# Three gate products in banks of their own, and the attention inputs' scale and bias on other engines

## The chip, the core and the metric

One core of one Trainium2 chip runs the whole program. The metric is the device time of one execution in microseconds (us), the median of three runs. All data are fp32 unless said otherwise.

## The reference, cut to what matters

The input x has 8 batches, 512 time steps and 256 features; a conditioning vector has 256 features per batch. Four layers are added to x one after the other. The first two are recurrences over the 512 steps, and they are what the change touches, with the projections that begin the third:

```
x = x + rnn(x, cond)      # h = tanh(x_t Wx + b + h Wh)
x = x + lstm(x, cond)     # a = x_t Wx + b + h Wh; i, f, o = sigmoid of three quarters, g = tanh of the last
                          # c = f * c + i * g;  h = o * tanh(c)
x = x + attention(x, cond)  # hyperbolic: layer_norm(logmap0(x)), expmap0, then q, k, v =
                            # logmap0(xm) @ w + b, heads, softmax, a feed-forward layer
x = x + experts(x, cond)  # gating over 4 experts, the best 2 of them, and a shared one
```

In the kernel logmap0(xm) @ w is written as s1 * (z @ w): the row factor s1 comes out of the norm of z, and the bias is added behind it.

## The kernel before, in words

The program has two blocks. The first holds both recurrences, with all that prepares the attention beside them; the second holds attention and experts, batch by batch, and the diff leaves it alone.

**The recurrences** (`recurrences`) run in 520 slots. Slot i does step i of the RNN and step n = i - 8 of the LSTM (`LAG` = 8). A state has 256 units for 8 batches. The products turn it round: the state is the stationary operand, 8 to 32 columns wide, and the weights stream past it in four strips of 32 array columns (`products`, tile_position (0, 32 j)), so the result lies on 128 partitions. Each slot issues for the LSTM a product for the forget and input gates into psFI (128 wide), one for the candidate into psG (64 wide), and a joint one for the output gate and the RNN into psOR. At 32 rows per group of four slots, a bank serves four steps: its stationary operand grows from 8 to 32 columns, and the four steps' bias (copied by ScalarE, `bias_of_group`, `bias_of_pair`) and input products (`inputs_of_group`, `inputs_of_pair`) are put in ahead.

VectorE transposes the results in 32x32 blocks back to units on partitions (FIT, GT, oT, RT), multiplies f * c (line 240, `gw<-sFI,cc`), makes the new cell state with one scan (line 243), and multiplies o * tanh(c) into Hs (line 250) and once more into RH (line 251).
```
dve.wait_ge(sem["w"], n + 1)      # line 241: f * c is there
dve.wait_ge(sem["tG"], n + 1)     # line 242: tanh of the candidate is there
dve.tensor_tensor_scan(...)       # line 243
```

After its LSTM and RNN work each engine does one slot's worth of side work (`inputs_made(i)`, and `Q.scalar_slot` or `Q.vector_slot` for the first batch's heads).

**The attention's inputs** (`AttentionInputs`) are that side work. A chunk is 16 steps of 8 batches, 128 rows; 32 chunks follow each other 16 slots apart. o counts a chunk's slots from 0, and two chunks overlap (o = 16 + p of one is o = p of the next). PE transposes the rows back (o = 0, 1), ScalarE copies them (o = 1), VectorE takes the moments (o = 2: bn_stats, bn_aggr) and clips (o = 5), GpSimd computes an inverse tanh with pow and a polynomial (up to line 907, signal d; after VectorE's group at o = 9, which ends with line 841, up to line 921, signal rstd), VectorE centres and scales (o = 13, 14), ScalarE sums the squares of z (o = 15, line 620), GpSimd takes the root (line 924, signal nz), VectorE makes the row factor s1 (`row_factors`, o = 20, lines 687 to 693), PE transposes z (o = 18, 19) and multiplies it with w_q, w_k, w_v (o = 20 to 31, one 128x128 product per slot, line 782). VectorE then writes each third, psB * s1 + bias, to the tile qkv (o = 23, 27, 31, line 856), and SP stores the chunk. `row_factors` in chunks after `GATHERED` = 24 has one more wait ahead of its reciprocal (line 689).

The line numbers in this document are those of the kernel before, also for instructions that the change keeps. 

Of the kernel before, what the change touches and what calls it, by code (L numbers as in the profile page):

```python
# [9 lines left out]
fp32 = mybir.dt.float32  # L10
# [7 lines left out]
P = 128  # L18
# [47 lines left out]
class Recurrence:  # L66
# [14 lines left out]
    SIGNALS = ("FI", "G", "OR", "XX", "X1", "sFI", "tG", "sO", "tR", "tC", "bFI", "bG", "bOR", "fiT", "gT", "rT", "w", "c",  # L81
# [3 lines left out]
    def __init__(self, nc, ctx, mem):  # L85
# [13 lines left out]
        self.FIT, self.GT, self.RT = sb("FIT", [P, 2 * KC, 32]), sb("GT", [P, KC, 32]), sb("RT", [P, KC, 32])  # L99
# [3 lines left out]
        self.psFI, self.psOR = ([ps(f"{n}{i}", 128) for i in range(2)] for n in ("psFI", "psOR"))  # L103
        self.psG = [ps(f"psG{i}", 64) for i in range(2)]
# [3 lines left out]
def recurrences(nc, R, F, Q, A, W):  # L108
# [5 lines left out]
    F_I, G_, O_, R_, O_R = slice(0, 128), slice(128, 192), slice(192, 256), slice(256, 320), slice(192, 320)  # L114
# [13 lines left out]
    with nc.Block() as block:  # L128

        @block.tensor  # L130
        def _(pe):
# [27 lines left out]
            def inputs_of_group(g, bank, cols, seeded, raises=None):  # L159
                q = g - FIRST  # L160
                if not 0 <= q < PIECES:
                    return
                pe.wait_ge(sem[seeded], q + 1)
# [4 lines left out]
                last = products(bank[g % 2], lambda k: x[:, k, :], 32, R.wx, cols)  # L168
                if raises:
                    last.then_inc(sem[raises], 1)  # L170
# [4 lines left out]
            for bank in R.psOR + R.psFI + R.psG:  # L175
# [6 lines left out]
            for i in range(SLOTS):  # L182
                g, s, n = i // 4, i % 4, i - LAG
                if lstm(i):
# [3 lines left out]
                    products(R.psFI[g % 2], h, width, R.wh, F_I).then_inc(sem["FI"], 1)  # L188
# [30 lines left out]
        def _(dve):  # L219
# [9 lines left out]
            for i in range(SLOTS):  # L229
                g, s, n = i // 4, i % 4, i - LAG  # L230
                at_pair = 2 * NB * (i % 2)
                if lstm(i):
                    dve.wait_ge(sem["FI"], n + 1)
                    dve.transpose(flat(R.FIT), R.psFI[g % 2]).then_inc(sem["fiT"], 1)  # L234
                    dve.wait_ge(sem["G"], n + 1)
                    dve.transpose(flat(R.GT), R.psG[g % 2]).then_inc(sem["gT"], 1)
                    dve.wait_ge(sem["sFI"], n + 1)
# [3 lines left out]
                    dve.wait_ge(sem["w"], n + 1)  # L241
                    dve.wait_ge(sem["tG"], n + 1)
# [53 lines left out]
        def _(act):  # L296
# [26 lines left out]
            for i in range(SLOTS):  # L323
# [12 lines left out]
                if rnn(i):  # L336
                    act.wait_ge(sem["rT"], i + 1)
                    act.activation(r_of(i), R.RT[:, :, at_pair:at_pair + NB], ACT.Tanh).then_inc(sem["tR"], 1)  # L338
                if s == 0:
                    bias_of_group(g + 1, R.psFI, F_I, "bFI")  # L340
# [4 lines left out]
                else:  # L345
# [3 lines left out]
                inputs_made(i)  # L349
                Q.scalar_slot(act, i)  # L350
# [95 lines left out]
class AttentionInputs:  # L446
# [14 lines left out]
    SIGNALS = {"xT": 1, "xT_out": 1, "mv": 1, "X2": 1, "n": 1, "m": 1, "d": 1, "dk": 1, "rstd": 1, "z": 1, "zz": 1, "nz": 1, "zT": 1, "zT_out": 1, "qkv": 3, "qkv_out": 3,  # L461
               "x_st": 16, "qkv_st": 16}

    def __init__(self, nc, ctx, mem, A, W, x_dram, qkv_dram, ada_dram, mod_dram, last_rows):
# [13 lines left out]
        self.psA, self.psB = (mem.enter_context(nc.psum_tensor(n, [P, 512], fp32)) for n in ("psA", "psB"))  # L478
# [88 lines left out]
    def last_bank(self, n, banks):  # L567
        return (self.psB, banks[4], banks[5])[n][:, 0:D]

    def last_rows_back(self, pe, x2, x2_made):  # L570
        c = NCH - 1
        pe.wait_ge(x2_made, 4 * (c + 1))
        pe.wait_ge(*self.at("zT_out", c - 2))
# [109 lines left out]
    def row_factors(self, dve, c):  # L683
# [10 lines left out]
        if c < NCH - 2:  # L694
            C.link(made)
# [33 lines left out]
    def tensor_engine(self, pe, x2, x2_made):  # L729
        def slot(i):  # L730
# [7 lines left out]
            if 12 <= i < 24:  # L738
# [3 lines left out]
                if (half, k) == (0, 0):  # L742
                    if j == 1:
# [1567 lines left out]
```

## Time and profile before

| | |
|---|---|
| median of 3 runs | 2344.58 us (2342.88 to 2344.84) |
| the profiled execution | 2343.05 us, its span 2341.3 us |
| mean granted TensorE clock | 0.991 |
| busy: PE, VectorE, ScalarE, GpSimd | 94%, 68%, 54%, 24% of the span |
| LSTM steps | 512 |

Engines in the rows: PE is TensorE's matrix products, DVE is VectorE, ACT is ScalarE, POOL is GpSimd; a q behind a name is the engine's queue, an instruction that keeps it waiting but does no work. A row of the timeline gives start, duration, engine, line, operation, output<-inputs and the shapes; `x16` means sixteen instructions merged, from the first start to the last end. PE products are pipelined, so a group's duration is longer than the distance to the next group's start.

### The profile page before, as it was taken

Reading aid. Unit: us, or ns where it says so; the run is one execution under the profiler, and the core shown is the slowest. Engines: PE = TensorE matmul, PEld = TensorE weight load, DVE = VectorE, ACT = ScalarE, POOL = GpSimd, SP = SyncE. Lnnn points to the kernel's source line nnn. Section 1 sums busy time; section 2 is a strip of 40 time slices with the busy share of each in tenths; the row PEclk is TensorE's granted clock in tenths of the full one; section 3 lists DMA queues with packets and bytes.
Section 4 is the critical chain, followed back from the end, with each engine's and each line's share of the span. In section 5 each row is a group of like instructions: output and inputs, shape, how many; then the busy total and the mean of one; then the engine's idle time right before and its main releaser. Section 6 shows DMA issues by size and latency. Waiting matters only on the chain. (4 is left out here: it accounts for less than half of the span.)

```text
span 2341.3 us, 94850 instructions
## 1 busy us (share of the span) xinstructions
PE 2207.2 (94%) x39004; PEld 1452.3 (62%) x39004; DVE 1581.1 (68%) x7316; ACT 1257.8 (54%) x4381; POOL 560.5 (24%) x1178
## 2 busy tenths in 40 slices
PE   8899999999999999999987699999999999999999
PEld 6677777777777777777743256464646556464666
DVE  5777777777777777777747684765747576674530
ACT  4555555555555555555565664647575564656432
POOL 0222222242221422214223031322213131221100
PEclk9999999999999999999998899999999999999999
DMA  4111111101000000000010200303030120302020
GB/s 119 36 38 31 38 40 42 37 25 32 29 31 27 22 27 29 31 27 18 23 69 1 88 35 1 131 1 131 1 131 1 38 94 1 131 1 104 0 86 9
DMA packets 51874, 102.64 MB, mean 44 GB/s; under 512 B 10468, under 2 KB 33380, under 8 KB 47348
## 3 DMA queue, kind: packets, MB, share of 16 engines
q1 hardware_dynamic: 48036, 94.06, 11.8%
q8 instruction: 309, 5.06, 0.9%
q10 hardware_dynamic: 3408, 2.52, 0.4%
q14 instruction: 121, 0.99, 0.1%
HBM read 75.53 MB, written 21.04 MB: 41 GB/s over the span
## 5 line engine op out<-in xcount | busy, mean ns | idle before, releaser
L135 PE MATMUL psFI<-wh,Hs 128*8 128x128 f32 (+3 forms) x8192 | 324.7, 276 | 61.0 <-DVE Hs L250 47.8
L135 PE MATMUL psOR<-wh,RH 128*16 128x128 f32 (+3 forms) x8320 | 321.5, 272 | 2.2 <-ACT RH L338 2.0
L135 PEld LDWEIGHTS psFI<-wh,Hs 128*8 128x8 f32 (+3 forms) x8192 | 182.2, 99 | 179.3 <-DVE Hs L250 179.3
L2054 ACT ACTIVATE pexp<-bank 128x1024 f32<-128x1024 f32 x256 | 244.3, 1023 | 36.1 <-PE bank L1384 35.9
L338 ACT ACTIVATE RH<-RT 128x16 f32<-128x16 f32 x512 | 110.9, 217 | 261.5 <-DVE RT L254 261.5
L1262 PE MATMUL bank<-x3T,ew 128*128 128x512 f32 x512 | 238.7, 593 | 0.0
L234 DVE STREAM_TRANSPOSE FIT<-psFI 128x128 f32<-128x128 f32 x512 | 162.0, 316 | 101.0 <-PE psFI L135 98.4
L329 ACT ACTIVATE sFI<-FIT 128x32 f32<-128x32 f32 x512 | 118.6, 232 | 200.4 <-DVE FIT L234 195.5
L135 PE MATMUL psG<-wh,Hs 128*8 128x64 f32 (+3 forms) x8192 | 208.6, 219 | 0.4 <-issue 0.4
L135 PEld LDWEIGHTS psOR<-wh,RH 128*16 128x16 f32 (+1 forms) x8320 | 205.7, 104 | 4.8 <-ACT RH L338 3.7
L1276 PE MATMUL bank<-ew,hidden 128*128 128x256 f32 x864 | 201.0, 379 | 0.0
L1276 PEld LDWEIGHTS bank<-ew,hidden 128*128 128x128 f32 x864 | 163.5, 190 | 56.5 <-issue 38.7
L1962 ACT ACTIVATE hidden<-bank,eb1s 128x512 f32<-128x512 f32 x128 | 87.8, 686 | 198.1 <-PE bank L1262 195.8
L2126 POOL TENSOR_TENSOR hs<-hs,half 128x16 f32<-128x16 f32 x32 | 92.8, 2901 | 378.0 <-DVE hs L1801 378.0
L782 PE MATMUL psB<-wqkv,zrT 128*128 128x128 f32 x720 | 175.8, 326 | 0.0
L135 PEld LDWEIGHTS psG<-wh,Hs 128*8 128x8 f32 (+3 forms) x8192 | 174.8, 100 | 0.6 <-issue 0.6
L135 PE MATMUL psOR<-wx,XX 128*32 128x128 f32 (+1 forms) x4160 | 168.9, 278 | 2.6 <-DMA XX<-in_xT 2.6
L335 ACT ACTIVATE tC<-cc 128x16 f32<-128x16 f32 x512 | 111.3, 217 | 105.6 <-DVE cc L243 104.8
L782 PEld LDWEIGHTS psB<-wqkv,zrT 128*128 128x128 f32 x720 | 107.1, 188 | 72.9 <-issue 70.4
L1262 PEld LDWEIGHTS bank<-x3T,ew 128*128 128x128 f32 x512 | 96.3, 190 | 77.0 <-issue 72.2
L250 DVE TENSOR_TENSOR Hs<-oT,tC 128x16 f32<-128x16 f32 x512 | 90.2, 176 | 75.8 <-ACT tC L335 1.4
L240 DVE TENSOR_TENSOR gw<-sFI,cc 128x16 f32<-128x16 f32 x512 | 90.4, 176 | 72.4 <-ACT sFI L329 3.0
(366 smaller groups left out, 4227.9 us busy)
## 6 DMA issues: line engine op xcount, KB each, us to landing
ew<-in_ew SPq DMA_DIRECT2D x32, 1024.0 KB, 9.1
qkv_scratch<-qkvr SPq DMA_DIRECT2D x31, 384.0 KB, 2.8
big<-qkv_scratch SPq DMA_DIRECT2D x7, 1536.0 KB, 7.8
XX<-in_xT SPq DMA_DIRECT2D x31, 256.0 KB, 2.7
x_scratch<-xr SPq DMA_DIRECT2D x32, 128.5 KB, 2.4
x<-x_scratch SPq DMA_DIRECT2D x8, 514.0 KB, 9.7
ada<-ada_scratch SPq DMA_DIRECT2D x8, 512.0 KB, 8.5
out_x<-x SPq DMA_DIRECT2D x7, 512.0 KB, 3.3
```

The source lines that it names most:

```text
L135: last = pe.matmul(bank[32 * j:32 * j + width, :], state(k), weights[:, k, j, cols], start=False, stop=k == KC - 1, tile_position=(0, 32 * ...
L234: dve.transpose(flat(R.FIT), R.psFI[g % 2]).then_inc(sem["fiT"], 1)
L240: dve.tensor_tensor(second_scan(R.gw), second_scan(R.sFI[:, 0]), second_scan(R.cc), ALU.mult).then_inc(sem["w"], 1)
L250: dve.tensor_tensor(h_alone(i), o, R.tC[:, :, :], ALU.mult).then_inc(sem["hL"], 1)
L329: act.activation(R.sFI[:, :, :, 1].rearrange("p g (k b) -> p (g k) b", k=KC), R.FIT[:, :, at_four:at_four + NB], ACT.Sigmoid).then_inc(sem ...
L335: act.activation(R.tC[:, :, :], by_block(second_scan(R.cc)), ACT.Tanh).then_inc(sem["tC"], 1)
L338: act.activation(r_of(i), R.RT[:, :, at_pair:at_pair + NB], ACT.Tanh).then_inc(sem["tR"], 1)
L782: last = pe.matmul(self.psB[:, half * P:(half + 1) * P], self.zT[:, k, :], self.wqkv[:, k, n * D + half * P:n * D + (half + 1) * P], start ...
L1262: last = pe.matmul(bank(4 + i % 2), M.expert(n)[0][:, k, m * P:(m + 1) * P], M.x3T[:, k, :], start=k == 0, stop=k == KC - 1)
L1276: last = pe.matmul(y_bank(q), M.hidden[:, i % HIDDEN, q * P:(q + 1) * P], M.expert(n)[1][:, m, :], start=m == 0 and (y_bank == M.last_bank ...
L2054: up(act.activation(M.pexp[:, n % 2, 2 * pr:2 * pr + 2, :], M.PS[pr][:, :, :], ACT.Exp, scale=1.0 / math.sqrt(HD)), "exps")
L2126: pool.tensor_tensor(out, base, exponent, ALU.pow).then_inc(M.sem(name), 1)
```

## The change

- psFI becomes psF and psI, each with two banks of 64 columns, and FIT becomes FT and IT. Per LSTM step there are three products of 64 columns in the order F, I, G, three transposes, and two sigmoids (F, I) in place of one. f * c waits for the sigmoid of F alone; the scan waits for f * c, the sigmoid of I and the candidate's tanh, in this order.
- Both halves of psG share one bank, so the G products wait in one slot of four for the bias copy, and the G input products for the transpose (gT).
- ScalarE does biases (but for the last of four slots) and side work ahead of `RH<-RT`, no longer behind it.
- psA and psB share one bank. The transposes and products of the attention's inputs are issued in four strips each.
- The chunk's thirds are scaled by ScalarE (Identity with scale s1) at o = 23, 27, 31, and GpSimd adds the bias, 128x256, in place (`biased`), behind lines 907, 921 and 924 of the next chunk's work. `row_factors` gets a wait on the scaled outputs of the chunk before.

```diff
@@ __init__
-        self.psFI, self.psOR = ([ps(f"{n}{i}", 128) for i in range(2)] for n in ("psFI", "psOR"))
-        self.psG = [ps(f"psG{i}", 64) for i in range(2)]
+        self.psF, self.psI = ([ps(f"{n}{i}", 64) for i in range(2)] for n in ("psF", "psI"))
+        self.bothG = ps("psG", 128)
+        self.psG = [self.bothG[:, 64 * i:64 * i + 64] for i in range(2)]
+        self.psOR = [ps(f"psOR{i}", 128) for i in range(2)]
@@ tensor engine, each slot
-                    products(R.psFI[g % 2], h, width, R.wh, F_I).then_inc(sem["FI"], 1)
+                    products(R.psF[g % 2], h, width, R.wh, F_).then_inc(sem["FI"], 1)
+                    products(R.psI[g % 2], h, width, R.wh, I_).then_inc(sem["FI"], 1)
+                    if s == 2 and g + 1 - FIRST < PIECES:
+                        pe.wait_ge(sem["bG"], g + 2 - FIRST)
                     products(R.psG[g % 2], h, width, R.wh, G_).then_inc(sem["G"], 1)
...
-                    inputs_of_group(g + 1, R.psFI, F_I, "bFI")
+                    inputs_of_group(g + 1, R.psF, F_, lambda q: (sem["bFI"], 2 * q + 1))
+                    inputs_of_group(g + 1, R.psI, I_, lambda q: (sem["bFI"], 2 * q + 2))
                 elif s == 2:
-                    inputs_of_group(g + 1, R.psG, G_, "bG", "X1")
+                    if lstm(i):
+                        pe.wait_ge(sem["gT"], n + 1)
+                    inputs_of_group(g + 1, R.psG, G_, lambda q: (sem["bG"], q + 1))
@@ vector engine
-                    dve.wait_ge(sem["FI"], n + 1)
-                    dve.transpose(flat(R.FIT), R.psFI[g % 2]).then_inc(sem["fiT"], 1)
+                    dve.wait_ge(sem["FI"], 2 * n + 1)
+                    dve.transpose(flat(R.FT), R.psF[g % 2]).then_inc(sem["fiT"], 1)
+                    dve.wait_ge(sem["FI"], 2 * n + 2)
+                    dve.transpose(flat(R.IT), R.psI[g % 2]).then_inc(sem["fiT"], 1)
                     dve.wait_ge(sem["G"], n + 1)
                     dve.transpose(flat(R.GT), R.psG[g % 2]).then_inc(sem["gT"], 1)
-                    dve.wait_ge(sem["sFI"], n + 1)
+                    dve.wait_ge(sem["sFI"], 2 * n + 1)
...
                     dve.wait_ge(sem["w"], n + 1)
+                    dve.wait_ge(sem["sFI"], 2 * n + 2)
                     dve.wait_ge(sem["tG"], n + 1)
@@ scalar engine
-                    act.wait_ge(sem["fiT"], n + 1)
-                    act.activation(R.sFI[:, :, :, 1].rearrange("p g (k b) -> p (g k) b", k=KC), R.FIT[:, :, at_four:at_four + NB], ACT.Sigmoid).then_inc(sem["sFI"], 1)
+                    act.wait_ge(sem["fiT"], 2 * n + 1)
+                    act.activation(by_block(second_scan(R.sFI[:, 0])), R.FT[:, :, at_four:at_four + NB], ACT.Sigmoid).then_inc(sem["sFI"], 1)
+                    act.wait_ge(sem["fiT"], 2 * n + 2)
+                    act.activation(by_block(second_scan(R.sFI[:, 1])), R.IT[:, :, at_four:at_four + NB], ACT.Sigmoid).then_inc(sem["sFI"], 1)
...
-                if rnn(i):
-                    act.wait_ge(sem["rT"], i + 1)
-                    act.activation(r_of(i), R.RT[:, :, at_pair:at_pair + NB], ACT.Tanh).then_inc(sem["tR"], 1)
                 if s == 0:
-                    bias_of_group(g + 1, R.psFI, F_I, "bFI")
+                    bias_of_group(g + 1, R.psF, F_, "bFI")
+                    bias_of_group(g + 1, R.psI, I_, "bFI")
...
+                inputs_made(i)
+                Q.scalar_slot(act, i)
+                if rnn(i):
+                    act.wait_ge(sem["rT"], i + 1)
+                    act.activation(r_of(i), R.RT[:, :, at_pair:at_pair + NB], ACT.Tanh).then_inc(sem["tR"], 1)
+                if s == 3:
                     if lstm(i):
                         act.wait_ge(sem["oT"], n + 1)
                     bias_of_pair(2 * g + 3)
-                inputs_made(i)
-                Q.scalar_slot(act, i)
@@ AttentionInputs
-        self.psA, self.psB = (mem.enter_context(nc.psum_tensor(n, [P, 512], fp32)) for n in ("psA", "psB"))
+        self.ps = mem.enter_context(nc.psum_tensor("psAB", [P, 512], fp32))
+        self.psA, self.psB = self.ps[:, 0:D], self.ps[:, D:2 * D]
@@ row_factors
+        if 0 < c < NCH - 1:
+            dve.wait_ge(*self.at("qkv_scaled", c - 1))
         dve.wait_ge(C.sem, C.n)
         C.link(dve.reciprocal(s1, nz))
@@ its tensor engine
+        def strips(out, stationary, moving, start, stop):
+            for j in range(4):
+                at = slice(32 * j, 32 * j + 32)
+                last = pe.matmul(out[at], stationary[:, at], moving, start=start, stop=stop, tile_position=(0, 32 * j), skip_group_check=True)
+            return last
...
-                    last = pe.transpose(self.psA[:, k * P:(k + 1) * P], self.z[:, k * P:(k + 1) * P], self.W.I[:, :])
+                    last = strips(self.psA[:, k * P:(k + 1) * P], self.z[:, k * P:(k + 1) * P], self.W.I[:, :], True, True)
...
-                    last = pe.matmul(self.psB[:, half * P:(half + 1) * P], self.zT[:, k, :], self.wqkv[:, k, n * D + half * P:n * D + (half + 1) * P],
-                                     start=k == 0, stop=k == KC - 1, skip_group_check=True)
+                    last = strips(self.psB[:, half * P:(half + 1) * P], self.zT[:, k, :], self.wqkv[:, k, n * D + half * P:n * D + (half + 1) * P],
+                                  k == 0, k == KC - 1)
@@ its scalar engine
+                if o in (23, 27, 31):
+                    third = (o - 23) // 4
+                    act.wait_ge(*self.at("qkv", c, third + 1))
+                    if third == 0:
+                        act.wait_ge(*self.at("s1", c))
+                        if c:
+                            act.wait_ge(*self.at("qkv_st", c - 1))
+                    cols = slice(third * D, (third + 1) * D)
+                    self.raise_(act.activation(self.qkv[:, cols], self.psB, ACT.Identity, scale=self.S[:, 13:14]), "qkv_scaled")
@@ its vector engine
-                if o in (23, 27, 31):
...
-                    self.raise_(dve.scalar_tensor_tensor(self.qkv[:, cols], self.psB[:, 0:D], s1, self.bqkv[:, cols], ALU.mult, ALU.add), "qkv_out")
@@ its GpSimd
+        def biased(chunk, third):
+            if 0 <= chunk < NCH - 2:
+                cols = slice(third * D, (third + 1) * D)
+                pool.wait_ge(*self.at("qkv_scaled", chunk, third + 1))
+                self.raise_(pool.tensor_tensor(self.qkv[:, cols], self.qkv[:, cols], self.bqkv[:, cols], ALU.add), "qkv_out")
...
             self.raise_(pool.tensor_tensor(d, t, a, ALU.mult), "d")
+            biased(c - 1, 0)
...
             self.raise_(pool.tensor_tensor(rstd, t, a, ALU.mult), "rstd")
+            biased(c - 1, 1)
...
             self.raise_(pool.tensor_tensor(nz, zz, half, ALU.pow), "nz")
+            biased(c - 1, 2)
```

## Rows read from the trace of the kernel before

**Rows 1.** One line's instructions: count, ns min/median/max, first and last start.

```profile
L234 DVE STREAM_TRANSPOSE FIT<-psFI x512: 294/317/318, 17.6 to 1182.8; 128x128 f32<-128x128 f32 x171
```

**Rows 2.** Timeline of one slot, all engines (start us, duration us).

```profile
603.50 0.63 PE L135 MATMUL psFI<-wh,Hs 128*16 128x128 f32 x16
...
603.95 0.41 PE L135 MATMUL psG<-wh,Hs 128*16 128x64 f32 x16
...
604.17 0.62 PE L135 MATMUL psOR<-wh,RH 128*32 128x128 f32 x16
604.20 0.32 DVE L234 STREAM_TRANSPOSE FIT<-psFI 128x128 f32<-128x128 f32 x1 [0.40 <-PE psFI L135]
604.44 0.23 DVE L236 STREAM_TRANSPOSE GT<-psG 128x64 f32<-128x64 f32 x1
...
604.71 0.22 ACT L331 ACTIVATE gw<-GT 128x16 f32<-128x16 f32 x1
...
604.82 0.18 DVE L240 TENSOR_TENSOR gw<-sFI,cc 128x16 f32<-128x16 f32 x1
...
605.03 0.23 DVE L243 TENSOR_TENSOR_SCAN cc<-sFI,gw 128x32 f32<-128x32 f32 x1
...
605.29 0.22 ACT L335 ACTIVATE tC<-cc 128x16 f32<-128x16 f32 x1 [0.20 <-DVE cc L243]
605.54 0.17 DVE L250 TENSOR_TENSOR Hs<-oT,tC 128x16 f32<-128x16 f32 x1
...
605.77 0.64 PE L135 MATMUL psFI<-wh,Hs 128*24 128x128 f32 x16
```

**Rows 3.** The instruction in VectorE's queue at line 242.

```profile
L242 DVEq EVENT_SEMAPHORE  x512: 21/21/21, 18.3 to 1183.6; - x171
```

**Rows 4.** Timeline of VectorE: row_factors of an earlier and of a late chunk.

```profile
576.47 0.14 DVE L687 TENSOR_SCALAR Sr<-Sr 128x1 f32<-128x1 f32 x1
576.65 0.16 DVE L691 RECIPROCAL Sr<-Sr 128x1 f32<-128x1 f32 x1
576.84 0.16 DVE L693 SCALAR_TENSOR_TENSOR Sr<-Sr 128x1 f32<-128x1 f32 x1
576.95 0.32 DVE L234 STREAM_TRANSPOSE FIT<-psFI 128x128 f32<-128x128 f32 x1
...
1049.78 0.14 DVE L687 TENSOR_SCALAR Sr<-Sr 128x1 f32<-128x1 f32 x1
1050.03 0.16 DVE L691 RECIPROCAL Sr<-Sr 128x1 f32<-128x1 f32 x1
```

**Rows 5.** Timeline of PE, VectorE and GpSimd: the group at o = 9.

```profile
587.61 0.42 PE L135 MATMUL psFI<-wh,Hs 128*24 128x128 f32 x8
...
588.21 0.15 DVE L841 TENSOR_SCALAR Sr<-Sr 128x1 f32<-128x1 f32 x1
...
593.53 0.19 POOL L921 TENSOR_TENSOR Sr<-Sr 128x1 f32<-128x1 f32 x1
```

**Rows 6.** Timeline: the squares and the root of a chunk; a scaling behind the recurrence.

```profile
601.79 0.41 ACT L620 ACTIVATE dumpr<-zr 128x256 f32<-128x256 f32 x1
...
602.43 0.55 POOL L924 TENSOR_TENSOR Sr<-Sr,half 128x1 f32<-128x1 f32 x1 [8.70 <-ACT dumpr L620]
...
1197.99 0.84 ACT L715 ACTIVATE big<-psG,Sr 128x256 f32<-128x256 f32 x2
```

**Rows 7.** One line's instructions: a 128x256 addition on GpSimd.

```profile
L726 POOL TENSOR_TENSOR spl<-spl,big x3: 717/722/722, 1204.4 to 1205.7; 128x256 f32<-128x256 f32 x3
```

**Rows 8.** Timeline of VectorE and GpSimd in two slots.

```profile
566.25 0.62 POOL L1095 TENSOR_TENSOR vt<-big,hs 128x256 f32<-128x256 f32 x1
566.57 0.33 DVE L250 TENSOR_TENSOR Hs<-oT,tC 128x16 f32<-128x16 f32 x1
...
618.62 0.19 POOL L907 TENSOR_TENSOR Sr<-Sr 128x1 f32<-128x1 f32 x1
618.64 0.25 DVE L243 TENSOR_TENSOR_SCAN cc<-sFI,gw 128x32 f32<-128x32 f32 x1
```

More of the change, by code:

```diff
@@ L167, in inputs_of_group @@
                 x = piece_of(R.x1, q)
-                last = products(bank[g % 2], lambda k: x[:, k, :], 32, R.wx, cols)
-                if raises:
-                    last.then_inc(sem[raises], 1)
+                products(bank[g % 2], lambda k: x[:, k, :], 32, R.wx, cols)
             inputs_made = F.tensor_engine(pe, lambda c: R.x2[c % 2], sem["x2"])
             pe.wait_ge(sem["zeroed"], 1)
-            for bank in R.psOR + R.psFI + R.psG:
+            for bank in R.psOR + R.psF + R.psI + [R.bothG]:
                 last = pe.matmul(bank, R.zero[:, :], R.zero[:, 0:bank.shape[1]], start=True, stop=True)
@@ L567, in last_bank @@
     def last_bank(self, n, banks):
-        return (self.psB, banks[4], banks[5])[n][:, 0:D]
+        return banks[4 + n][:, 0:D]
     def last_rows_back(self, pe, x2, x2_made):
@@ L694, in row_factors @@
         if c < NCH - 2:
-            C.link(made)
+            self.raise_(made, "s1")
         else:
@@ L742, in slot @@
                 if (half, k) == (0, 0):
-                    if j == 1:
-                        pe.wait_ge(self.mod_made, 1)
-                    if j == 2:
-                        pe.wait_ge(self.ada_made, 1)
-                bank = (self.psB, self.psA)[j % 2]
-                last = pe.matmul(bank[0:NB, half * 256:(half + 1) * 256], self.cond[:, k, :], self.wada[:, k, j * 512 + half * 256:j * 512 + (half + 1) * 256],
+                    pe.wait_ge(*((self.ada_made, j) if j else (self.mod_made, 1)))
+                last = pe.matmul(self.ps[0:NB, half * 256:(half + 1) * 256], self.cond[:, k, :], self.wada[:, k, j * 512 + half * 256:j * 512 + (half + 1) * 256],
                                  start=k == 0, stop=k == KC - 1, skip_group_check=True)
@@ L756, in slot @@
                         if c == 0:
-                            pe.wait_ge(self.ada_made, 2)
+                            pe.wait_ge(self.ada_made, 3)
                         if c >= 2:
-                            pe.wait_ge(*self.at("zT_out", c - 2))
+                            pe.wait_ge(*self.at("qkv_scaled", c - 2))
                     columns = self.psA[:, 0:D].rearrange("p (j k u) -> p j k u", k=KC, u=32)[:, :, o, :]
-                    last = pe.transpose(columns, x2(c)[:, o, :], self.W.I[:, :])
+                    last = strips(columns, x2(c)[:, o, :], self.W.I[:, :], True, True)
                     if o == 1:
@@ L806, in vector_engine @@
         C = self.vector
-        m, d, k, small, e, s1 = (self.S[:, i:i + 1] for i in (1, 5, 6, 9, 10, 13))
+        m, d, k, small, e = (self.S[:, i:i + 1] for i in (1, 5, 6, 9, 10))
         def slot(i):
@@ L820, in slot @@
                 dve.wait_ge(self.ada_ps, j + 1)
-                bank, cols = (self.psB, self.psA)[j % 2], slice(j * 512, (j + 1) * 512)
+                bank, cols = self.ps, slice(j * 512, (j + 1) * 512)
                 dve.tensor_tensor(self.ada[:, cols], bank[0:NB, :], self.ada[:, cols], ALU.add).then_inc(self.ada_made, 1)
@@ L1117, in kept_busy @@
         for _ in range(n):
-            pe.matmul(self.F.psA[:, :], self.F.wqkv[:, 0, 0:P], self.F.wqkv[:, 1, 0:512], start=True, stop=True)
+            pe.matmul(self.F.ps[:, :], self.F.wqkv[:, 0, 0:P], self.F.wqkv[:, 1, 0:512], start=True, stop=True)
     def last_transposes(self, pe):
```

24 lines of the change are left out of this document (8 added, 16 removed).

## The prediction, made before the changed kernel ran

> **What bounds the kernel now.** The first view to read is one instruction that runs once per LSTM step. The forget-and-input transpose runs 512 times, from 17.6 to 1182.8 us [rows 1]: (1182.8 - 17.6) / 511 = 2.280 us per step, and the recurrence is half of the span. The diff touches only this half; its end moves the rest along with it.
>
> The second view is one slot of the timeline, in which every start is explained by one earlier end [rows 2]. Counted from the start of the psFI products at 603.50: psG starts at 0.45 and ends at 0.86, its transpose GT starts at 0.94, the candidate's tanh (gw<-GT) ends at 1.43, the scan starts at 1.53, tanh of the cell (tC) at 1.79, Hs at 2.04, the next psFI at 2.27. A second branch runs beside it: psFI ends at 0.63, FIT starts at 0.70, and by way of the sigmoid the product gw<-sFI starts at 1.32 and ends at 1.50. So two branches meet at the scan: it starts 0.10 after the candidate's tanh has ended and 0.03 after the product has.
>
> Which of the two holds it? The usual latency between engines is 0.03 to 0.04 (GT ends at 604.67, the tanh starts at 604.71; tC ends at 605.51, Hs starts at 605.54). But the scan has two waits, and the second (line 242, on tG) is an instruction of its own in VectorE's queue, 21 ns long [rows 3]. What such a second wait costs is shown by L691: with one wait it starts 0.04 after L687 has ended, and in a late chunk, where line 689 adds a wait, 0.11 after it [rows 4]. So a chain that arrives by the second wait needs about 0.10, which is just what the scan needs behind the candidate's tanh. **Both branches bind at the same moment**, to within 0.01 us. That decides my sum: shortening only the product's branch gains nothing.
>
> **The change, part by part.**
>
> *F, I, G in own banks.* A 128-wide burst takes 0.45 from its start to the next start, a 64-wide one 0.22 [rows 2]. F, I and G start at 0, 0.22 and 0.45, and I allow 0.01 for two short bursts in place of a long one, so the candidate's product ends 0.01 later than now. Its transpose now starts 0.08 after it, behind a FIT that is 0.32 long; FIT itself started 0.07 after its product. With two short transposes ahead, GT should need 0.07 too. Net 0.00 to 0.01 earlier; I take 0.005: 512 x 0.005 = **-2.6 us**. The forget gate is early by 0.2 (F ends at 0.42, FT runs 0.49 to 0.72, its sigmoid to 0.98, the product follows GT at 1.09), so the product ends at 1.27 instead of 1.50, and for nothing: the scan still waits for the tanh by its last wait, 0.10. The sigmoid of I (0.97 to 1.19) clears ScalarE just ahead of the tanh at 1.20.
>
> *VectorE's side work.* It runs between the x-additions and the first transpose, which is due at 0.70 now and at 0.49 afterwards. Work of a chunk that ran until 0.70 for nothing now pushes FT, IT and GT. GT started 0.08 before FIT had ended, so a transpose of 0.23 frees its successor after 0.15 [rows 2], and FT loses nothing if it can start by 0.94 - 2 x 0.15 = 0.64. The chunk's row_factors ends with L693, 0.11 ahead of FIT and so 0.59 into its slot [rows 4]; the new wait on qkv_scaled makes its reciprocal a two-wait instruction, 0.07 later, and FT comes at 0.74: loss 0.10 to 0.14. The o = 9 group ends with L841, which starts 0.60 into its slot [rows 5]: FT at 0.68, loss 0.04 to 0.08. The bn_stats group loses 0.00 to 0.03. Sum 0.14 to 0.25, I take 0.20: 31 x 0.20 = **+6.2 us**. The three outputs that leave VectorE (L856) gain nothing where they end before FIT, as they do now; they would have cost after it, which the change avoids.
>
> *ScalarE's order.* ScalarE has nothing to do from the issue of tC (1.79) to RH<-RT, 0.2 into the next slot; biases and side work now fill this gap. What must not be late is tR, which the psOR products need at 0.67 [rows 2]. In most slots the added work (up to 0.48) ends before RT does. Only in the slot with o = 31 and o = 15 are there a scaling of 0.48 and the squares [rows 6], and tR ends near 0.66, some 0.04 late for psOR; sO and oT have 0.1 to spare before Hs. Zero, and 30 x 0.1 = 3 us if that spare is gone. The strips save PE time in the second half of a slot, where PE waits for Hs anyway: zero. The bank shared by psA and psB adds waits on outputs scaled 16 slots earlier: zero.
>
> *The bias on GpSimd.* Three 128x256 additions per chunk, for 30 chunks. The nearest in form, L726, takes 0.72 us [rows 7]; the multiplication L1095 takes 0.62. GpSimd has room for them. But look at VectorE beside L1095 [rows 8]: Hs started at 566.57, inside 566.25 to 566.87, and lasted 0.33 where the others last 0.17. It ended 0.03 after GpSimd had ended. Hs, with both inputs in SBUF, was held to GpSimd's end and the slot grew by 0.15. For the scan, which has two SBUF inputs as well, no row shows a wide neighbour; beside the small L907 it took 0.25 in place of 0.23 [rows 8, 2], so something holds it too, and I treat it as Hs. So the question is where the three additions fall:
> 1. biased(c-1, 1) follows L921. L921 ends 593.72 - 588.36 = 5.36 after L841 does, which is 0.75 into its slot [rows 5]; two slots on (2.33, with FT late, and 2.27) this is 0.75 + 5.36 - 4.60 = 1.51. The addition runs from 1.60 to 2.32. Hs would end at 2.20 and ends at 2.35 or, if the scan (from 1.51) first delays GpSimd, at 2.43: 0.15 to 0.23, I take 0.19.
> 2. biased(c-1, 2) follows L924. In the o = 15 slot ScalarE scales the last third from 1.94; two such in a row take 0.84, so the next starts 0.36 after the first, and the squares run from 2.30. L924 starts 0.64 after them and takes 0.55 [rows 6]: 2.94 - 2.28 = 0.66 to 1.21 of the next slot. The addition: 1.29 to 2.01. The scan, due from 1.51 to 1.74, ends at 2.04 (1.94 if the addition takes 0.62): 0.20 to 0.30, I take 0.25.
> 3. biased(c-1, 0) waits for ScalarE, which ends at 2.42: it runs from 0.29 to 1.01 of the next slot. There VectorE has transposes from PSUM only, and none of those is seen to grow. Zero.
> Sum 30 x 0.44 = **+13.2 us**; bounds 0 (all fall beside) and 30 x 3 x 0.7 = 63 (all held in full).
>
> Beside [rows 8] stands a rule of the Trainium skill ("SBUF — State Buffer", Who interferes with whom): a VectorE instruction with two SBUF inputs and a GpSimd instruction that reads SBUF exclude each other for its whole length. For Hs the trace agrees (0.33 against 0.17). It would hold the scan as well and so leaves the sum as it is; by the scan's own row alone (0.02 longer) the second addition would cost 0.6 us in place of 7.5, and the sum would be 7 us lower.
>
> **Sum.** -2.6 + 6.2 + 13.2 = +16.8. The profiled execution took 2343.05 us (span 2341.3 and 1.75 around it), 1.5 below the median of 2344.58. Against the median: **2361 us**. Its own range, from the terms' bounds: -5 to 0, +5 to +8, 30 x (0.36 to 0.53) = +11 to +16, so +11 to +24, 2355 to 2369. I call 0.2%, 4.7 us, the least that a measurement can tell from no change.
>
> **Rivals.**
> *The product's branch was the real bound* (0.18; the other side). The scan's 0.03 after the product is as short as any; if the tanh's 0.10 were slack, it could start at 1.43 + 0.03 = 1.46 instead of 1.53. 512 x 0.07 = 36 us off, 2361 - 36 = 2325. It decides as soon as the last wait costs less than 0.06. Against it stands L691 [rows 4].
> *GpSimd's additions fall beside* (0.15). If their start is off by some 0.4 and GpSimd runs between RT and GT instead, +3.6 remains: 2348, no change that can be told.
> *They collide more* (0.13). If the first addition meets the gw product or the scan as well, and each costs 0.4 to 0.5: 30 x 1.35 = 40 in place of 13: 2388.
> *The likeliest* has 0.54. To hold 8 in 10, the range takes the first, third and part of the others: 2338 to 2380. Faster 0.19, same 0.14, slower 0.67.
>
> **What would show it.** Right: in a plain slot the scan starts 0.10 after gw<-GT ends, while gw<-sFI has ended 0.2 earlier, and the period stays 2.26 to 2.27; one slot in 16 has an Hs, another a scan, of 0.35 to 0.55, ending 0.03 after a GpSimd addition; FT late after L693 and L841. Wrong: a scan at 0.03 to 0.06 behind the tanh and a period near 2.19; or additions lying between RT and GT. A late RH<-RT or a PE that can't keep up 0.22 per burst over three in a row would make it slower than I say.

## The result, and the profile after

The changed kernel takes 2612.94 us (median of 4 runs, 2609.16 to 2617.28) against 2344.71 us (4 runs, 2342.88 to 2345.86) of the kernel before: ratio 1.1145, 95% interval 1.1126 to 1.1165, or 268 us slower. The forecast was 2361 us with a range of 2338 to 2380: the direction was right, the size wrong by 252 us. The granted clock is 0.99 in both profiled executions, so TensorE's clock has no part in it. One of the four runs of or_split_wx below took 5452 us, which nothing here explains; it is left out, and its other three took 2356 to 2358 us.

In what follows an "instruction of PE" is a weight load or a matmul, and a "pair" is one of each. The rows of a run carry that run's own line numbers; line numbers in the text without a row are those of the kernel before.

The page of the kernel after: PE's busy share (94% before), its matmuls (39004 before), the queue that moves instructions, and the rows of PE's products. The last row is that of psG in the kernel before.

```profile
span 2610.8 us, 122758 instructions
...
PE 2163.5 (83%) x52260; PEld 1524.1 (58%) x52260; DVE 1607.7 (62%) x7738; ACT 1425.6 (55%) x5111; POOL 626.1 (24%) x1268
...
q8 instruction: 414, 6.78, 1.1%
...
L137 PE MATMUL psOR<-wh,RH 128*16 128x128 f32 (+3 forms) x8320 | 359.2, 274 | 46.5 <-issue 44.6
L137 PE MATMUL psF<-wh,Hs 128*8 128x64 f32 (+3 forms) x8192 | 233.6, 223 | 182.3 <-DVE Hs L259 155.6
...
L137 PE MATMUL psG<-wh,Hs 128*8 128x64 f32 (+3 forms) x8192 | 238.5, 220 | 46.0 <-issue 45.9
L137 PE MATMUL psI<-wh,Hs 128*8 128x64 f32 (+3 forms) x8192 | 234.5, 220 | 39.2 <-issue 39.0
```

```profile
L135 PE MATMUL psG<-wh,Hs 128*8 128x64 f32 (+3 forms) x8192 | 208.6, 219 | 0.4 <-issue 0.4
```

PE has a third more matmuls, and as many more weight loads, and is nevertheless busy for a smaller share of a longer time. The last column says what it was idle for. psF, the first product of a slot, waits for Hs, as psFI did. At psG, psI and psOR it is not another engine but "issue", that is, nothing that the profile shows. In the kernel before psG's products waited 0.4 us; now it is 46 us, and 39 and 45 at psI and psOR. A matmul takes what it took (220 ns at 64 columns, 274 at 128).

The timeline of after shows where such idle time lies. Start, duration, engine, line; in brackets the idle time before and who ended it.

```profile
704.51 0.18 DVE L259 TENSOR_TENSOR Hs<-oT,tC 128x16 f32<-128x16 f32 x1
...
704.74 0.31 PE L137 MATMUL psF<-wh,Hs 128*24 128x64 f32 x8 [0.33 <-DVE Hs L259]
...
705.76 0.31 PE L137 MATMUL psF<-wh,Hs 128*24 128x64 f32 x8 [0.71 <-issue]
705.89 0.41 PE L137 MATMUL psI<-wh,Hs 128*24 128x64 f32 x16
...
706.14 0.25 DVE L240 STREAM_TRANSPOSE FT<-psF 128x64 f32<-128x64 f32 x1 [0.98 <-PE psF L137]
...
707.96 0.43 PE L137 MATMUL psF<-wh,Hs 128*32 128x64 f32 x16 [0.56 <-DVE Hs L259]
```

Eight of the sixteen products of the forget gate run as soon as Hs is there, then PE stands still for 0.71 us in the middle of the burst, with no wait on a semaphore, and the other eight run. FT starts 1.40 us into the slot, where the median is 0.50, and the slot lasts 707.96 - 704.74 = 3.22 us. Between 100 and 1100 us there are 235 places where PE starts nothing for over 0.25 us with no wait on the next instruction (210 us in all); before there are none. Counted in all that PE's queue holds, weight loads and waits included, they lie 256 apart (the 5th percentile, the median and the 75th are all 256; some are 512 apart), and all 235 stand at the same place of a block of 256. The queue of instructions moves blocks of 6.78 MB / 414 = 16.4 KB. That it is PE's follows from the count: 414 x 256 = 105984, and PE has 105942 entries with its waits. In the 9 us around this stall it moves three blocks:

```profile
DMA  2000000000000000003000000000000000020000
GB/s 73 0 0 0 0 0 0 0 0 0 0 0 0 0 0 0 0 0 73 0 0 0 0 0 0 0 0 0 0 0 0 0 0 0 0 73 0 0 0 0
...
q8 instruction: 3, 0.05, 2.2%
```

(703 to 712 us in 40 slices: blocks at 703.0, 707.1 and 710.9.) A stall ends 1.4 us after a block has landed (the middle 80% lie between 1.25 and 1.50). So PE runs out of instructions once per block. It is fed 256 per 3.9 us or so, and the kernel now asks for more. The windows view counts it, 400 to 500 us, first before, then after (us, then busy time and instructions of PE, PEld, VectorE, ScalarE and GpSimd; at the end the clock, the DMA share and GB/s):

```profile
400.00:500.00 100.00, 95.84 (x2894) 71.31 (x2892) 77.02 (x431) 52.69 (x278) 29.38 (x83) 1.00 0.13 37
```

```profile
400.00:500.00 100.00, 73.31 (x3239) 61.80 (x3227) 62.03 (x369) 52.88 (x268) 26.99 (x85) 1.00 0.13 36
```

57.9 instructions per us before, 64.7 after, although the slots are longer. An LSTM step issues 66 pairs of weight load and matmul before (each product of the program becomes two pairs here: 24 products with wh and 8 with wx make 64, and 2 belong to the attention's inputs) and 92 after: 32 products with wh (64 pairs), 10 with wx (20), and the strips 8. Over 432 slots in the middle the step takes 2.816 us, 184 / 2.816 = 65.3 per us. Two thirds of these slots have a stall in them and take 3.01 us on average, the others 2.39.

The Trainium skill speaks of it ("Runtime: NRT & Kernel Launch", Instruction fetch mechanics): instructions come in blocks of 16 KiB, 256 of them, and crossing a border costs a step that is "mostly hidden". The trace agrees on the block, 256 and 16.4 KB, and disagrees on the cost here, 210 us of stalls in 1000 us.

### The profile page after: what moved, and what is told of

It is laid out like the page before. It is cut to its first block and busy times, and to the rows that moved or that the text cites. A ratio compares the mean times of both kernels' runs of the same rounds, so it can differ in the third digit from the quotient of the medians.

```text
span 2610.8 us, 122758 instructions
## 1 busy us (share of the span) xinstructions
PE 2163.5 (83%) x52260; PEld 1524.1 (58%) x52260; DVE 1607.7 (62%) x7738; ACT 1425.6 (55%) x5111; POOL 626.1 (24%) x1268
## 3 DMA queue, kind: packets, MB, share of 16 engines
q8 instruction: 414, 6.78, 1.1%
## 5 line engine op out<-in xcount | busy, mean ns | idle before, releaser
L137 PE MATMUL psOR<-wh,RH 128*16 128x128 f32 (+3 forms) x8320 | 359.2, 274 | 46.5 <-issue 44.6
L137 PE MATMUL psF<-wh,Hs 128*8 128x64 f32 (+3 forms) x8192 | 233.6, 223 | 182.3 <-DVE Hs L259 155.6
L137 PEld LDWEIGHTS psF<-wh,Hs 128*8 128x8 f32 (+3 forms) x8192 | 142.2, 99 | 280.4 <-DVE Hs L259 244.5
L137 PE MATMUL psI<-wh,Hs 128*8 128x64 f32 (+3 forms) x8192 | 234.5, 220 | 39.2 <-issue 39.0
L338 ACT ACTIVATE sFI<-FT 128x16 f32<-128x16 f32 x512 | 111.7, 218 | 234.2 <-DVE FT L240 233.7
L252 DVE TENSOR_TENSOR_SCAN cc<-sFI,gw 128x32 f32<-128x32 f32 x512 | 118.6, 232 | 156.6 <-ACT gw L342 156.0
L240 DVE STREAM_TRANSPOSE FT<-psF 128x64 f32<-128x64 f32 x512 | 126.5, 247 | 117.8 <-PE psF L137 114.5
L137 PEld LDWEIGHTS psI<-wh,Hs 128*8 128x8 f32 (+3 forms) x8192 | 162.0, 100 | 49.5 <-issue 49.5
L748 PE MATMUL psAB<-wqkv,zrT 128*32 128x128 f32 x2880 | 170.1, 274 | 10.3 <-issue 10.3
L244 DVE STREAM_TRANSPOSE GT<-psG 128x64 f32<-128x64 f32 x512 | 126.9, 248 | 58.3 <-PE psG L137 58.0
```

The lines of the kernel that those rows point to most:

```text
L137: last = pe.matmul(bank[32 * j:32 * j + width, :], state(k), weights[:, k, j, cols], start=False, stop=k == KC - 1, tile_position=(0, 32 * ...
L240: dve.transpose(flat(R.FT), R.psF[g % 2]).then_inc(sem["fiT"], 1)
L252: dve.tensor_tensor_scan(R.cc[:, :, :].rearrange("p u i -> p (u i)"), R.sFI[:, 1].rearrange("p u i -> p (u i)"), R.gw[:, :, :].rearrange(" ...
L338: act.activation(by_block(second_scan(R.sFI[:, 0])), R.FT[:, :, at_four:at_four + NB], ACT.Sigmoid).then_inc(sem["sFI"], 1)
L748: last = pe.matmul(out[at], stationary[:, at], moving, start=start, stop=stop, tile_position=(0, 32 * j), skip_group_check=True)
```

## The experiments

**1. The change without its three products, and without its strips.** The side work stays: ScalarE scales, GpSimd adds the bias, ScalarE's order and the shared bank. The shared bank that stays is that of psA and psB; psG has two banks again, without the added waits. side_only keeps the strips, side_nostrips doesn't.

```
- products(R.psF[g % 2], h, width, R.wh, F_).then_inc(sem["FI"], 1)
- products(R.psI[g % 2], h, width, R.wh, I_).then_inc(sem["FI"], 1)
+ products(R.psFI[g % 2], h, width, R.wh, F_I).then_inc(sem["FI"], 1)
  (one transpose FIT, one sigmoid; side_nostrips: pe.transpose and pe.matmul on 128 columns for strips(...))
```

> The kernel after with forget and input gates in one product, one transpose and one sigmoid again; the strips, ScalarE's scaling, GpSimd's bias, the order on ScalarE and the shared bank stay. Theory A (PE's instruction supply: the trace of after shows a PE stall every 256 instructions once they come faster than some 65 per us): about 72 pairs of weight load and matmul per slot, 144 instructions, 2.21 us at 65.3 per us, so below the 2.28 us of a slot: no limit, and the time is that of my sum without its first term, 2344.7 + 6.2 + 13.2 = 2364, at most 2370; only bursts of side products may stall. Theory B (the strips themselves, their tiling or the side work, cost most of the 268 us): over 2450.

> As side_only, and the attention's products and transposes on the full array again: what is left of the change is ScalarE's scaling, GpSimd's bias, ScalarE's order and the shared bank. About 66 pairs per slot as before, 132 instructions. Instruction supply: no difference from side_only beyond some bursts, so 2350 to 2366; if GpSimd's collisions with VectorE are what I priced, above 2357; if the additions fall beside it, 2345 to 2352.

side_only 2366.13 us, ratio 1.0106 (1.0089 to 1.0123), 72 pairs per slot; side_nostrips 2362.12 us, 1.0085 (1.0068 to 1.0102), 66 pairs. Before, measured beside them: 2342.45. So the side work costs 20 us, the strips 4 us as long as PE is below its supply (7 stalls in 1000 us), and the rest of the 268 us is not there without the third product. Where the 20 us go shows in two slots of sixteen of side_nostrips:

```profile
610.17 0.62 PE L136 MATMUL psFI<-wh,Hs 128*8 128x128 f32 x16
...
610.81 0.55 POOL L937 TENSOR_TENSOR Sr<-Sr,half 128x1 f32<-128x1 f32 x1 [7.54 <-ACT dumpr L620]
...
611.33 0.73 POOL L882 TENSOR_TENSOR qkvr<-qkvr,bqkv 128x256 f32<-128x256 f32 x1
...
611.48 0.61 DVE L239 TENSOR_TENSOR gw<-sFI,cc 128x16 f32<-128x16 f32 x1
...
612.12 0.23 DVE L242 TENSOR_TENSOR_SCAN cc<-sFI,gw 128x32 f32<-128x32 f32 x1
...
639.72 0.75 POOL L882 TENSOR_TENSOR qkvr<-qkvr,bqkv 128x256 f32<-128x256 f32 x1
...
640.19 0.32 DVE L249 TENSOR_TENSOR Hs<-oT,tC 128x16 f32<-128x16 f32 x1
```

The product w takes 0.61 in place of 0.18 and ends at 612.09, 0.03 behind the addition; Hs takes 0.32 in place of 0.18, again until GpSimd has ended. The first slot is 0.43 longer for it (2.689 against 2.256), the second 0.13 (2.393 against 2.258), and so it is in every chunk: 30 x 0.56 = 17 us.

**2. The three products without the strips.** after_nostrips: the kernel after with pe.transpose and pe.matmul on the full array in place of strips(...).

> The kernel after with its products and transposes for the attention on the full array again. Instruction supply: 64 + 20 + 2 = 86 pairs per slot instead of 92, 172 instructions, at 65.3 per us 2.63 us per slot: 512 x (2.804 - 2.634) = 87 us less than after, about 2526 us. Rival (the drains of the strips and their columns cost the time): below 2400. Rival (a longer chain of three gate products and three transposes, strips nothing): about 2610 as after.

2538.58 us, 86 pairs per slot, a step of 2.657 us: 12 us above the expectation. The rate is 64.5 per us, under the 65.3 that I had taken, and 171 stalls remain. Strips cost 74 us here and 4 us in side_only: their price depends on what PE's supply already carries.

**3. More instructions for the same work, in the kernel before.** The joint product of output gate and RNN is issued in two halves: same columns, banks and waits.

```
-                    return products(psOR, state, width, weights, O_R)
+                    products(psOR[:, 0:64], state, width, weights, O_)
+                    return products(psOR[:, 64:128], state, width, weights, R_)
```

or_split_all does it everywhere, or_split_wh only where weights is R.wh, or_split_wx only where it is R.wx.

> The kernel before with one edit: the joint product of output gate and RNN (128 columns) issued as two of 64 columns, of the state and of the inputs. The same columns, banks, waits and results, but 24 more pairs per slot: 90 pairs, 180 instructions. Instruction supply: 180 / 65.3 = 2.76 us per slot over 504 slots that have both, so 2344.7 + 504 x (2.76 - 2.28) = about 2585 us, with stalls every 256 instructions. Rival (array time or the chain of gates sets it): the split product lies beside the work of VectorE and ScalarE, 2345 to 2375 us.

> The kernel before with the joint product of output gate and RNN split in two of 64 columns for the state alone, the input products left joint: 16 more pairs per slot, 82 pairs, 164 instructions. Instruction supply: 164 / 65.3 = 2.51 us per slot, 2344.7 + 504 x (2.51 - 2.28) = about 2461 us. A cost for each added pair that is the same whatever their rate would give two thirds of the 235 us of the full split, 2502.

> The kernel before with the joint product of output gate and RNN split in two of 64 columns for the inputs alone: 8 more pairs per slot on average, 74 pairs, 148 instructions, 2.27 us per slot at 65.3 per us, just under the 2.28 of a slot. Instruction supply with a ceiling: few stalls, 2345 to 2356. A cost that grows with each added pair from the first on (84 us for 16 of them): about 2387.

or_split_all 2577.82 us, or_split_wh 2426.07, or_split_wx 2357.11 (ratio 1.0061, 1.0041 to 1.0081). From the windows view of or_split_all, 400 to 500 us, and from its page:

```profile
400.00:500.00 100.00, 85.10 (x3330) 68.69 (x3330) 65.09 (x359) 43.81 (x231) 19.75 (x69) 1.00 0.12 33
```

```profile
L135 PE MATMUL psOR<-wh,RH 128*16 128x64 f32 (+1 forms) x16384 | 374.8, 221 | 90.3 <-issue 87.9
L135 PEld LDWEIGHTS psOR<-wh,RH 128*16 128x16 f32 (+1 forms) x16384 | 290.2, 104 | 109.9 <-issue 105.7
L135 PE MATMUL psG<-wh,Hs 128*8 128x64 f32 (+3 forms) x8192 | 237.4, 220 | 33.5 <-issue 33.2
```

psG's products, which nobody touched, now wait 33 us for "issue" where they waited 0.4 us before. With no third product, no strip, no new bank and no GpSimd addition, the kernel before has the stalls of the kernel after, 256 instructions apart. What each kernel issues and takes, over the same 432 slots:

| kernel | pairs per slot | slot, us | instructions per us | stalls over 0.25 us, 100 to 1100 us |
|---|---|---|---|---|
| before | 65.8 | 2.278 | 57.7 | 0 |
| few_inputs (experiment 4) | 68.2 | 2.358 | 57.9 | 1 |
| few_inputs_tG_first (experiment 4) | 68.2 | 2.264 | 60.3 | 5 |
| side_only | 72.0 | 2.322 | 62.0 | 7 |
| or_split_wx | 73.8 | 2.303 | 64.0 | 22 |
| or_split_wh | 81.7 | 2.443 | 66.9 | 117 |
| after_nostrips | 85.8 | 2.657 | 64.5 | 171 |
| or_split_all | 89.7 | 2.748 | 65.3 | 212 |
| after | 92.0 | 2.816 | 65.3 | 235 |

The ceiling holds for the two with the most instructions to 0.1. It is not a sharp one: or_split_wx, at 64.0, has 22 stalls (10 us of the 14 that it lost), after_nostrips has 171 at a mean of 64.5, and or_split_wh gets 66.9, so it came out 35 us below the expectation. I missed there by taking one rate for all; why that kernel is fed 2% faster stays open. The stalls of all these kernels stand at the same place of a block of 256.

**4. The three products below the ceiling.** few_inputs is after_nostrips with seven of eight products with wx left out, 68 pairs per slot. few_inputs_tG_first moves one wait in it.

```
+                        if weights is R.wx and (k, j) != (KC - 1, 3):
+                            continue
...
+                    dve.wait_ge(sem["tG"], n + 1)      (few_inputs_tG_first)
                     dve.wait_ge(sem["w"], n + 1)
                     dve.wait_ge(sem["sFI"], 2 * n + 2)
-                    dve.wait_ge(sem["tG"], n + 1)
```

> The kernel after with its products and transposes for the attention on the full array, and of each input product of the recurrences (eight matmuls of wx) only the last one issued: seven eighths of the input products are left out, so its gates are other numbers. Forget, input and candidate gates stay in three products, banks and transposes. 64 + 2.5 + 2 = about 69 pairs per slot instead of 86. Instruction supply: 138 instructions, 2.11 us at 65.3 per us, below the chain's 2.27 to 2.30: the stalls go, slots are like the unstalled ones of after (2.29 at the fastest), and with the collisions of GpSimd measured before (20 us) the time is 2355 to 2385. Rival (three products and three transposes make the chain itself long): above 2450. Rival (my first term, the own banks win 0.005 per slot): about 2360.

> As few_inputs, with the same part left out, and the three waits ahead of the scan in another order: the candidate's tanh first, then the product w, then the input gate's sigmoid. My theory that a scan starts 0.10 behind the wait written second and later ones but 0.03 behind the first one: the tanh ends last in these slots, so the scan starts 0.06 to 0.07 earlier, 512 x 0.065 = 33 us less than few_inputs, about 2335 to 2350. Rival (the 0.10 is a property of ScalarE's result on its way to VectorE, not of the wait's place): no difference.

few_inputs 2384.21 us, few_inputs_tG_first 2336.47 us. Of after_nostrips' time 154 us went with the input products, and one stall is left. The edit takes away the products' time on the array too, but that was not what cost: in after_nostrips the slots with no stall in or just before them, the two with GpSimd's collisions aside, have a median of 2.308 us with all the input products, and those of few_inputs have 2.306. So the 154 us were supply. Nor does psG's shared bank with its waits, which few_inputs keeps, cost anything: its plain slots are 0.036 us longer than those of before in all four slots of a group, with that bank's waits in one of them. A plain slot of few_inputs, then the same slot of the other (the candidate's tanh, the scan, tC, Hs):

```profile
630.46 0.41 PE L139 MATMUL psF<-wh,Hs 128*8 128x64 f32 x16 [0.40 <-DVE Hs L261]
...
631.38 0.25 DVE L246 STREAM_TRANSPOSE GT<-psG 128x64 f32<-128x64 f32 x1
...
631.56 0.14 DVE L250 TENSOR_TENSOR gw<-sFI,cc 128x16 f32<-128x16 f32 x1
631.67 0.22 ACT L344 ACTIVATE gw<-GT 128x16 f32<-128x16 f32 x1
...
632.01 0.22 DVE L254 TENSOR_TENSOR_SCAN cc<-sFI,gw 128x32 f32<-128x32 f32 x1 [0.32 <-ACT gw L344]
```

```profile
608.21 0.41 PE L139 MATMUL psF<-wh,Hs 128*8 128x64 f32 x16 [0.31 <-DVE Hs L261]
...
609.41 0.22 ACT L344 ACTIVATE gw<-GT 128x16 f32<-128x16 f32 x1
...
609.66 0.23 DVE L254 TENSOR_TENSOR_SCAN cc<-sFI,gw 128x32 f32<-128x32 f32 x1 [0.22 <-ACT gw L344]
```

The scan starts 632.01 - 631.89 = 0.12 after the tanh has ended, and 609.66 - 609.63 = 0.03 in the other (medians 0.130 and 0.033). The gain is 0.097 per plain slot, not 0.065, since three waits and not two were ahead of this scan. The trace shows where they stand: the wait that is written first goes with the scan itself (in the kernel before that for w), and the others precede it in one instruction of the queue. So it isn't, as was said of the kernel before, the wait just before an instruction that goes with it, and further waits needn't be an instruction each. The queue's instruction in front of this scan holds two waits and is 50 ns long, where that of before holds one and is 21 [rows 3]:

```profile
L253 DVEq EVENT_SEMAPHORE  x512: 49/50/50, 18.2 to 1223.8; - x171
```

**5. The order of the waits in the kernel before.** The lines 241 and 242 exchanged, w second.

> The kernel before with the two waits ahead of the scan exchanged: the candidate's tanh first, the product w second. In before w ends 0.036 ahead of the scan and the tanh 0.100 ahead of it. If the 0.10 belongs to the place of the wait, the product, which ends 0.064 later than the tanh, now has it too: 512 x 0.064 = 33 us slower, 2375 to 2380. If it belongs to the engine that signals, no change: 2342 to 2347.

2376.31 us, ratio 1.0144 (1.0127 to 1.0160): 34 us for two exchanged lines. The product w (VectorE's own result) ends at 629.13 and the scan starts 0.11 behind it (median 0.10), where it was 0.03:

```profile
628.86 0.22 ACT L331 ACTIVATE gw<-GT 128x16 f32<-128x16 f32 x1
...
628.96 0.17 DVE L240 TENSOR_TENSOR gw<-sFI,cc 128x16 f32<-128x16 f32 x1
...
629.24 0.22 DVE L243 TENSOR_TENSOR_SCAN cc<-sFI,gw 128x32 f32<-128x32 f32 x1
```

So the price belongs to the place of the wait and not to the engine that signals.

**6. The same order in the kernel after.** after_tG_first: the edit of few_inputs_tG_first in the kernel after.

> The kernel after with the tanh's wait ahead of the waits for w and for the input gate before the scan, the order that made the slots 0.07 to 0.09 shorter where few input products were issued (48 us). If PE's instruction supply sets the slot of after, its 184 instructions per slot still take 2.81 us: 2600 to 2613, no gain. If the chain of the gates sets it and the stalls only add to it, 35 to 50 us less: 2565 to 2580.

2615.56 us against 2612.94 of the kernel after: nothing gained. In its fastest slots the scan does come early (they take 2.19 us; those of after 2.29), and the mean slot is 2.82 us all the same, at 65.2 instructions per us. The chain that the change was to shorten isn't what sets the time after.

**7. GpSimd's additions.** Both are edits of side_nostrips. side_one_column leaves the bias out of all columns but the first of each third; side_quarters does the whole addition in four instructions.

```
- pool.tensor_tensor(self.qkv[:, cols], self.qkv[:, cols], self.bqkv[:, cols], ALU.add)      (256 columns)
+ the same on one column (side_one_column), or four times on 64 columns (side_quarters)
```

> side_nostrips with each of GpSimd's additions of the bias cut from 256 columns to one: the bias is left out of all other columns of the attention's inputs. If the 20 us of side_nostrips over before are VectorE's collisions with those additions (in its trace w takes 0.61 instead of 0.18 in one slot of sixteen, Hs 0.31 in another), they go: 2341 to 2348. If the tail of GpSimd's queue, the scaling on ScalarE or ScalarE's new order cost them, about 2362 stays. My sum's other term, 6 us for VectorE's side work beside GpSimd's small operations, would leave 2348 to 2351.

> side_nostrips with each of GpSimd's additions issued as four of 64 columns. If one instruction of GpSimd keeps VectorE waiting for its own length at most (an addition of 256 columns takes 0.73 us), a quarter keeps it for some 0.25 and VectorE gets in between: the 20 us of side_nostrips over before shrink to 5 to 12, 2347 to 2354. Rival: the four follow each other so closely that VectorE waits for all of them, 2362 or more.

side_one_column 2345.52 us, ratio 1.0013 (1.0004 to 1.0023); side_quarters 2349.76 us, 1.0028 (1.0017 to 1.0038), before 2342.85. The additions cost 2362.12 - 2345.52 = 17 us, and all else in the side work 3 us. In quarters they take longer in sum, and VectorE gets in between:

```profile
644.64 1.15 POOL L884 TENSOR_TENSOR qkvr<-qkvr,bqkv 128x64 f32<-128x64 f32 x4
...
644.79 0.20 DVE L239 TENSOR_TENSOR gw<-sFI,cc 128x16 f32<-128x16 f32 x1
...
645.03 0.29 DVE L242 TENSOR_TENSOR_SCAN cc<-sFI,gw 128x32 f32<-128x32 f32 x1
...
645.61 0.22 DVE L249 TENSOR_TENSOR Hs<-oT,tC 128x16 f32<-128x16 f32 x1
```

w 0.20, the scan 0.29 and Hs 0.22 in place of one w of 0.61: 0.14 lost in this slot and not 0.43, and nothing in the slot where Hs was held.

## Why the prediction was wrong in size

**The step that failed** is a term that the sum didn't have: "The strips save PE time in the second half of a slot, where PE waits for Hs anyway: zero", and the three bursts at "0.22" from start to start. Both were costed by the array's time. The term that is missing is what PE's instruction supply takes, and for the strips it was put at nothing. On that supply they are not free: 132 instructions per slot became 184, 40% more, of which the third product brings 40 and the strips 12. A slot then lasts 184 / 65.3 = 2.82 us, whatever the chain does. The last sentence of the prediction named it ("a PE that can't keep up"), but as a case without a price or a chance. The profile of before held the numbers to ask the question: 39004 pairs, a queue of instructions that moves them in 309 blocks, a rate of 57.7 per us. It could not hold the answer, since no 100 us of before go faster than 58.1 per us, and the sum should have had a wide upper bound for a change that adds 40% to the instructions of the busiest engine.

How the 268 us divide, by differences between runs: the side work 20 (2362.12 - 2342.45); the longer chain and its collisions 22 (few_inputs - side_nostrips); supply with the third product 154 (after_nostrips - few_inputs); the strips on top 74 (after - after_nostrips). Sum 270; supply is 228 of it. few_inputs and after_nostrips ran once each, so a difference with them is good to some 5 us (an estimate from the kernels that ran more often, whose runs lie 3 to 8 us apart).

**F, I and G in own banks (-2.6 us).** Measured without the ceiling: a plain slot takes 2.293 where it took 2.257, so +0.036, 18 us, and in the other direction. The candidate's product ends 0.01 later and its transpose starts 0.07 behind it, both as forecast. The transpose takes 0.25, not 0.23, but the tanh ends only 0.01 later than before. What I missed are 0.03 us at the scan: I looked at "its last wait, 0.10" and didn't count that the split sigmoid adds a third wait, which lengthens the instruction in front of the scan. In the kernel after it starts 745.32 - 745.19 = 0.13 behind the tanh:

```profile
744.97 0.22 ACT L342 ACTIVATE gw<-GT 128x16 f32<-128x16 f32 x1
...
745.32 0.22 DVE L252 TENSOR_TENSOR_SCAN cc<-sFI,gw 128x32 f32<-128x32 f32 x1 [0.33 <-ACT gw L342]
```

**Both branches bind at the scan.** Right, and the strongest part of the argument: swap_waits costs 0.066 per slot, against 0.064 expected, and the rival ("the product's branch was the real bound", 2325 us) is refuted: the product's branch did come 0.25 earlier (few_inputs: w ends at 631.70, the scan starts at 632.01) and nothing followed.

**VectorE's side work (+6.2 us).** Mis-sized. FT did start at 0.74 in the slot with row_factors, as worked out; it cost 0.06 in few_inputs, not 0.10 to 0.14, and the other slots lost nothing (few_inputs: FT at 0.66 and 0.61 and 0.63 in three more slots of sixteen, none of them longer than its neighbours by over 0.01). 31 x 0.06 = 1.9 us.

**ScalarE's order (0) and the shared bank (0).** Right: with the additions cut, all of the side work left costs 3 us.

**GpSimd's collisions (+13.2 us).** The mechanism was right and the size near: 17 us in side_nostrips. One addition met Hs as forecast (it ran from 1.55 of its slot, forecast 1.60; the slot grew by 0.13, forecast 0.19). The other was 0.13 earlier than forecast (1.16, not 1.29), and that put it on w, which was held for its whole length, instead of the scan: 0.43, not 0.25. A GpSimd instruction starts right behind the one before it, where I had allowed 0.08. The rule of the Trainium skill that was weighed ("SBUF — State Buffer", Who interferes with whom) is borne out by w, which reads two inputs in SBUF (0.61 against 0.18). It isn't for GpSimd's narrow operations: in the kernel before 31 products w begin inside a 128x1 operation of 0.55 us, most of them with 0.4 us of it still to run, and none takes over 0.18.

The sum for the kernel without the third product was 2344.7 + 6.2 + 13.2 = 2364, and side_only measured 2366: the work that was priced was priced about right, and the bound that replaced it was not on the list.

## What to carry to other kernels

Count the instructions of the busiest engine before and after a change that splits operations, and divide by the time of a step: in these runs PE is fed with hardly a stall at 58 to 60 instructions per us, stalls more and more from 62 on and gets no more than 65 to 67. "Idle until issue" on an engine with nothing to wait for, at every 256th instruction, is the sign, and a split or a strip that is nearly free below that rate costs its full share above it. Ahead of an instruction of VectorE with several waits write the one that ends last first: 34 and 48 us lay in one line's place. No version faster than the kernel before came out of this: the order with the tanh first gains 0.06 per slot over before only with three products, and those don't fit under the ceiling unless the input products, which the result needs, are left out.

## What the runs showed of the hardware that I had not expected

- PE's instructions come in blocks of 256, 16.4 KB each. In after, or_split_all and after_nostrips one block follows the other by 3.83 to 3.85 us (median; one in twenty by less than 3.5), although the fetch itself takes 1.1 us (median, before and after alike). In the kernel after a stall ends 1.4 us (median) behind the landing of a block. What fills the rest of the 3.8 us isn't shown by any row here and stays open.
- It isn't the matmuls' width that sets the rate: 64-column and 128-column bursts stall alike, and two kernels with different work (after, or_split_all) have the same 65.3 per us. But the count isn't all either, since or_split_wh gets 66.9.
- The wait written first goes with the instruction; the second and the third share one instruction in the queue ahead of it, of 21 ns with one wait and of 50 ns with two. When the last signal is one of theirs, the scan starts 0.10 and 0.13 after it; when it is that of the first wait, 0.03.
